# Products of constants on TensorE at the phase ends, phase starts and attention openings of a six-phase transformer kernel

## What is computed

```
x = x + 0.5 * ffn0(layernorm(x))      # f1: 256 -> 704 -> 256, quantised weights
x = x + attn0(layernorm(x))           # a2: 16 heads of 16, rotary, not causal
x = x + 0.5 * ffn0(layernorm(x))      # f3: as f1
x = x + 0.5 * ffn1(layernorm(x))      # d4: 32 experts (top 4, at most 128 tokens each) and a shared expert
x = x + attn1(layernorm(x))           # a5: 16 heads, causal, with a position bias
x = x + 0.5 * ffn1(layernorm(x))      # d6: as d4
```

## Time and profile before

| | us |
|---|---|
| runs before: median (lowest to highest of 3) | 3001.02 (2999.36 to 3005.0) |
| the profiled execution: its own time | 3007.55 |
| its span, first to last instruction | 3005.8 |
| PE busy in the span | 2670.5 (89%) |
| DVE / ACT / POOL busy | 1951.0 / 1263.7 / 657.4 |
| mean granted TensorE clock | 0.945 |

### The profile page before, as it was taken

The page is one execution under the profiler, slowest core; times in us unless marked ns, Lnnn a source line. Parts: engine busy times, 40 slices in busy tenths (PEclk is TensorE's granted clock), DMA queues, the critical chain, the costliest instruction groups (busy, mean ns, idle before and its releaser), DMA issues. The chain is left out here.

```text
span 3005.8 us, 40300 instructions
## 1 busy us (share of the span) xinstructions
PE 2670.5 (89%) x14292; PEld 1280.2 (43%) x14292; DVE 1951.0 (65%) x4227; ACT 1263.7 (42%) x1901; POOL 657.4 (22%) x640
## 2 busy tenths in 40 slices
PE   3985899999999999797999994699999999799997
PEld 2442233333333332354455662344444544455554
DVE  5875887887877886485774334567667674576333
ACT  1431355655655657543211221155555556221321
POOL 0540331231321400153002431212111100000342
PEclk8997799999999999998999997799999999899998
DMA  3003321303303200001202653633233330300566
GB/s 115 1 1 79 64 43 28 59 20 51 59 17 48 51 15 1 1 1 64 87 32 49 142 125 85 108 57 62 45 65 65 60 54 2 105 32 26 119 140 165
DMA packets 161155, 175.78 MB, mean 58 GB/s; under 512 B 19186, under 2 KB 132786, under 8 KB 160818
## 3 DMA queue, kind: packets, MB, share of 16 engines
q1 hardware_dynamic: 144388, 151.26, 22.8%
q0 software_dynamic: 12416, 17.84, 3.6%
q10 hardware_dynamic: 4160, 4.19, 0.4%
HBM read 116.32 MB, written 56.13 MB: 57 GB/s over the span
## 5 line engine op out<-in xcount | busy, mean ns | idle before, releaser
L1744 DVE TENSOR_REDUCE a_mx<-a_bank 128x1 f32<-128x512 f32 (+3 forms) x1792 | 1032.4, 628 | 327.7 <-PE a_bank L1494 249.9
L1626 ACT ACTIVATE a_E<-a_bank 128x1024 f32<-128x1024 f32 (+3 forms) x896 | 795.8, 932 | 430.5 <-PE a_bank L1549 298.4
L1494 PE MATMUL a_bank<-a_KT,a_QT 96*128 96x512 bf16 (+4 forms) x1792 | 582.2, 371 | 89.2 <-DMA a_KT<-parts 50.5
L1549 PE MATMUL a_bank<-a_QT,a_KT 99*128 99x512 bf16 (+4 forms) x1792 | 511.7, 361 | 12.9 <-DMA a_QT<-a_mT 10.5
L1564 PE MATMUL a_bank<-a_E,a_Vg 128*32 128x512 f32 (+3 forms) x3584 | 442.0, 565 | 0.7 <-ACT a_E L1626 0.7
L1494 PEld LDWEIGHTS a_bank<-a_KT,a_QT 96*128 96x128 bf16 (+1 forms) x1792 | 151.0, 98 | 571.3 <-DVE a_mx L1744 295.6
L1549 PEld LDWEIGHTS a_bank<-a_QT,a_KT 99*128 99x128 bf16 (+1 forms) x1792 | 171.2, 99 | 190.6 <-ACT a_E L1626 34.3
L848 PE MATMUL d_bank<-wdT,d_hT 128*128 128x256 f32 (+1 forms) x768 | 202.6, 408 | 22.2 <-DVE x L1054 22.2
L960 ACT ACTIVATE d_silu<-d_bank 128x512 f32<-128x512 f32 x96 | 57.2, 596 | 380.8 <-PE d_bank L835 377.1
L1044 DVE SCALAR_TENSOR_TENSOR d_silu<-d_silu,d_bank 128x512 f32<-128x512 f32 x96 | 65.6, 683 | 232.3 <-ACT d_silu L960 232.2
L433 POOL TENSOR_TENSOR f_hl<-f_hT,f_hh 128x512 f16<-128x512 f32 x96 | 111.1, 1157 | 392.1 <-ACT f_hh L452 392.1
(11 more groups left out here) (224 smaller groups left out, 3624.3 us busy)
## 6 DMA issues: line engine op xcount, KB each, us to landing
parts<-a_parts SPq DMA_DIRECT2D x64, 384.0 KB, 2.5
a_QT<-parts SPq DMA_DIRECT2D x192, 128.0 KB, 5.4
a_KT<-parts SPq DMA_DIRECT2D x192, 128.0 KB, 8.4
d_wgu<-in_L_ffn_w_gate SPq DMA_DIRECT2D x64, 176.0 KB
d_wgu<-in_L_ffn_w_up SPq DMA_DIRECT2D x64, 176.0 KB
d_wd<-in_L_ffn_w_down SPq DMA_DIRECT2D x64, 176.0 KB
normalised<-d_xn SPq DMA_DIRECT2D x8, 1152.0 KB, 4.7
acc<-d_zero SPq DMA_DIRECT2D x66, 128.0 KB, 1.8
```

The lines of the kernel that those rows point to most:

```text
L1494: last = nc.tensor.matmul(out[:, 0:w], QT[0:W, h, qt * P:(qt + 1) * P], KT[0:W, h, kh * HALF:kh * HALF + w], start=True, stop=not diag)
L1549: last = nc.tensor.matmul(out, KT[:, h, kt * P:(kt + 1) * P], QT[:, h, half * HALF + c0:(half + 1) * HALF], start=True, stop=not diag)
L1626: nc.scalar.activation(E[:, u % 2, 2 * pair:2 * pair + 2, c0:HALF], bank[:, 2 * pair:2 * pair + 2, c0:HALF], ACT.Exp).then_inc(exps, 1)
L1744: nc.vector.tensor_reduce(mx[:, j, qt, kh:kh + 1], out[:, 0:w], AX.X, ALU.max).then_inc(freed_dve, 1)
```

## The change

`spin(out, n)` issues n matmuls of the f32 identity (stationary, 128x128) with 512 f32 columns of the kept constants (moving) into a PSUM tile that nobody reads. They wait for no semaphore and signal none. Nothing else is changed.

```diff
+    def spin(self, out, n):
+
+        for _ in range(n):
+            self.nc.tensor.matmul(out, self.const("ident"), self.consts[:, 0:4 * P], start=True, stop=True)
 
@@ ffn0_phase, TensorE
+                core.spin(down[:, 0, :], 2)
                 turn(0)
                 every(pe, chunk)
                 for i in range(CT):
                     down_proj(NCH - 1, 1, i)
+                core.spin(gate[:, 0, :], 4)
@@ mixture_phase, TensorE
+                core.spin(bank[:, 5, :], 2)
                 pe.wait_ge(s_in, START + 48)
                 pe.wait_ge(setup, START + 1)
...
                     for n in per_slot.get((c, j), ()):
                         expert_step(n)
+                core.spin(bank[:, 0, :], 4 if final else 24)
@@ attention_phase, TensorE
+                core.spin(bank[:, 4, :], 2)
                 if second:
                     pe.wait_ge(w_in, START + 32)
                 for x in opening:
+                    if x == ("chunk", 0):
+                        core.spin(bank[:, 4, :], 14)
                     fill(x)
...
                 for x in closing:
                     fill(x)
+                core.spin(bank[:, 0, :], 4)
```

## The result

| | before | with the change |
|---|---|---|
| median (lowest to highest), 13 runs each | 3003.6 (2992.8 to 3009.4) us | 3014.3 (3007.3 to 3017.0) us |
| ratio, 95% interval | | 1.003 (1.0018 to 1.0042) |
| the profiled execution: its own time, span | 3007.55, 3005.8 us | 3016.81, 3015.0 us |
| mean granted TensorE clock | 0.945 | 0.958 |

A forecast was written before the change was run, and what follows sets the result against it. TensorE, busy 89% of the span, was taken to bound the kernel. 12.6 + 3.0 + 0.3 - 1.0 = +14.9 us on the median 3001.02 gave 3015.9 us, 0.5% slower; range 3007 to 3021 us.

The forecast's parts named there:

- the likeliest case: Whole kernel: slower by more than 0.2% (6 us), chance 0.83.
- The price of a product: One f32 matmul of 512 columns on TensorE takes 0.86 us at the high clock, 1.72 us at the low.
- The rival of half the price: A product costs 0.43 us, so d4's end loses only 1.5 us; 3001.5 us in all, chance 0.06.
- the one in which TensorE does not hold up the barrier: d4's products run under the loading of a5's weights, or products miss the chip; about 3001 us, no change, chance 0.04.
- the one in which the clock stays down: At d4's end the products run at the low clock throughout: +31.6 us, so 3035 us; chance 0.03.
- The 24 at d4's end: 24 products outlast VectorE's readiness at the end of d4 and delay a5: +12.6 us, bounds +10.9 and +13.6.
- the 3.4 us of low clock: At d4's end the products first run 3.4 us more at the low clock, adding 1.7 us to 20.6.
- The 4s: 4 products at each other end: +1.0 in f1 and f3, +0.5 in a2 and a5, nothing in d6; +3.0 us.
- The starts: 2 products at each phase start hide under other work, except in a2, where they cost +0.3 us.
- The openings: 14 products in each attention opening (a2, a5) hide in the waits, leaving 15 and 11 us idle; cost 0.
- What the clock gives back: Hotter work behind the products: -1.0 us in a2, nothing in the openings, f3 and the mixtures.
- the clock stays up: Products carry the high clock over the barriers; some 30 us come back, less 15.9 of delay: 2987 us, chance 0.05.

The follow-up runs named there:

- the last version: Against the kernel before: 2 products at each start (5 in a5), 31 and 26 in the openings, none at ends; 2993.35 us, ratio 0.9957.

## Why the prediction was right, and what its size missed

The direction, the range and the likeliest case held: 3014.3 us lies within 3007 to 3021. It is 1.6 us below the 3015.9 that was named, but the kernel before was 2.6 us higher in these runs than in the three that the prediction had. Measured against the kernel before beside it the change is +9 (ratio) to +10.7 us (medians), and the sum said +14.9: two thirds of it. That the time came within 2 us of the one named is thus in part luck: the sum was too high, and the base too low. (The lower end of the range follows from 3001 + 7 as 3008, not 3007; and 5.78 us by twelve is 0.48 us a row, not 0.45. Neither matters.) Point by point:

- **The price of a product**, 0.86 us from `gate_up`'s rows: 0.864 by 48 of them, and 21.0 us in the time for 24 more. Right. The rival of half the price fell; so did the one in which TensorE does not hold up the barrier, and the one in which the clock stays down.
- **The 24 at d4's end**, +12.6: at the place itself +10.4 in the changed kernel and +13.1 alone. The step that I had sized from one execution is the mixture of slack and clock. The slack is longer where `down_proj` is hot (10.6 to 10.8 us in four of the profiles without products behind it, 9.7 in the kernel before). And the 3.4 us of low clock, worth 1.7, came from no row: the products ran cold for about 4 us in the kernel with the 24 alone, but not at all in the changed kernel nor in the one with 48, and there `down_proj` had been cold as well.
- **The 4s**, +3.0: about +3.4 at the places, 1.2 where 1.0 was said and 0.5 where 0.5 was. Right.
- **The starts**, +0.3 of cost: a2's first transposes come 3.1 us after the barrier where it was 2.9, so +0.2; the others hide, as said. Right for the changed kernel. In the three profiles with products at the starts and none at the ends the two are cold throughout (3.75 us), and it is +0.7, above the bound of 0.5.
- **The openings**: 15.77 and 10.88 us of idleness left, predicted 15 and 11, and the clock behind them unchanged. Right.
- **What the clock gives back**, -1.0: undersized. In the traces a2's opening is 39.2 - 37.9 = 1.3 us shorter, and d4 and d6 are 0.7 and 0.6 shorter up to their first `gate_up`. That is -2.6. The step that failed is "in f3 and the two mixtures ... I give them nothing": in the mixtures a gap of 0.55 us between the products and the transposes did not lose the level, and the 16 transposes take 2.50 to 2.71 us at all twelve mixture starts with products ahead, and 3.35 to 3.65 at all fourteen without. Up to the first `gate_up` that makes 9.8 us against 10.8 in the mean, but single ones lie anywhere between 7.9 and 11.4. For f3 the step held. The 33-column matmuls did stay cold for the most part in the changed kernel, as the prediction had it. What they take depends on where the level happens to change: 5.31 us in d4 of the last version, but also 5.36, 5.30 and 4.22 in d4 of three kernels with nothing ahead of them (48 at the end, openings filled, ends alone).
- **The wait for a5's weights** was no term of the change, but it is in the difference of the two profiles. From the first DMA to the first transposes it lasts 8.97 us in the profile of before and 6.98 in that of after. In the profiles of the eleven experiments it lies between 6.3 and 9.5, without regard to what was added. Of the 9.3 us between the two profiles, -2.0 are this.

The places add up: 10.4 + 3.4 + 0.2 - 2.6 - 2.0 = +9.4, of 9.2 us between the spans. The interiors of the phases moved as well, by up to 3 us, but about cancel; more of that below. What stays open: alone, the 24 products cost 13 us at their place in the profile and 5.4 to 10.5 in the timing. The profile was of the slowest execution, and in the changed kernel, with a hotter `down_proj`, the place cost 2.7 us less; no trace of another execution shows whether that is the whole of it.

The rule of the Trainium skill (TensorE: Matmul & The Clock Gate, HAM oscillation — how this bites in real kernels) that keeping the engine fed cures cold bursts, for which the rival "the clock stays up" stood, is borne out in one half by the traces. Where products ran up to the work (0.0 us of idleness between them in a2, 0.55 in the mixtures, 1.7 in a5's filled opening), the work was hot, wholly or in part. That was not so in f3 of the three profiles with products at the starts and none at the ends: the gap was 0.65 us, and the clock stayed at 0.50 (1.97 us). The rule did not carry the change. With 3.2 us between (a5's transposes, 3.98 us as before) and with 11 or 16 (the openings) nothing was gained, and the products at the ends, with the barrier behind them, show no gain by themselves.

## What to carry to other kernels

Work that nobody reads is free only as far as the engine's slack at the next meeting, and beyond it each microsecond is paid in full: read the slack off the drains and set the count by the measured price of that very type (f32 is four times bf16 here). It paid here only where it ran straight up to the work that was to be hot, ended before that work's data arrived, and hid under a wait, and even there not at every place (f3 got nothing from it); products at the end of a phase, ahead of a meeting, gave nothing. Judge such changes of 0.1 to 0.5% by timed rounds: single executions of this kernel differ by more.

## What was unexpected about the hardware

- A kernel can get slower while its mean clock rises: 0.945 to 0.958 with +0.3% of time, since the added products run mostly at the high clock, and the mean takes them in.
- Two products that themselves ran cold (3.75 us) were enough to take the 16 transposes behind them in d4 from 3.65 to 2.55 us. In f3 two such products, as near to the transposes, were not.
- Work that no edit touches does not take the same time twice: from its first group of chunks to the first transposes of f3, a2 takes between 905.6 and 915.6 us in the thirteen profiles (912.1 before, 915.6 with the change). Differences of 1 to 3 us between two profiles inside a phase therefore say nothing of an edit.
- The wait for the same weights after the same barrier varies between 6.3 and 9.5 us from one execution to another, which is a third of the effect that was studied.
